# Attention and GRU kernel: the order of the first norm's powers and of two groups' block products

## What is computed

```python
block_repr = x.reshape(B, 8, 4, 256).sum(axis=2)          # 8 blocks of 4 tokens
keys = block_repr @ Wk.T;  keys = keys / rms(keys) * rms_weight
attn = softmax(keys @ q)                                   # over the 8 blocks
attended = sum(attn * block_repr)                          # one row per sequence
y = layernorm(x + attended @ Wo.T) * ln_gamma + ln_beta
```

## Time and profile before

| | |
|---|---|
| median of 3 executions | 449.07 us |
| lowest, highest | 448.49, 478.3 us |
| profiled execution | 448.79 us, its span 447.0 us |
| PE, DVE, ACT, POOL busy | 95%, 73%, 55%, 25% of the span |
| granted TensorE clock | 0.999 of full speed |

### The profile page before, as it was taken

The page is one execution under the profiler, slowest core; times in us unless marked ns, Lnnn a source line. Parts: engine busy times, 40 slices in busy tenths (PEclk is TensorE's granted clock), DMA queues, the critical chain, the costliest instruction groups (busy, mean ns, idle before and its releaser), DMA issues.

```text
span 447.0 us, 13398 instructions
## 1 busy us (share of the span) xinstructions
PE 422.7 (95%) x5424; PEld 347.7 (78%) x5424; DVE 325.2 (73%) x985; ACT 244.3 (55%) x558; POOL 109.9 (25%) x122
## 2 busy tenths in 40 slices
PE   8879899999999999999999899999999999999994
PEld 6436587787777777777777688899999999999984
DVE  3597688798788887878868945666677766777665
ACT  6255748568576586765876553444444444444341
POOL 7682434435134251342525300000000000000000
PEclk9999999999999999999999999999999999999999
DMA  8941513313133131331213100001010000000001
GB/s 287 408 165 44 151 36 89 88 51 90 63 91 88 57 96 54 93 88 49 84 31 92 28 1 1 1 2 47 1 47 14 36 24 26 23 25 25 24 25 70
DMA packets 34268, 30.36 MB, mean 68 GB/s; under 512 B 4128, under 2 KB 29344, under 8 KB 34208
## 3 DMA queue, kind: packets, MB, share of 16 engines
q1 hardware_dynamic: 34208, 29.51, 20.4%
HBM read 16.92 MB, written 8.39 MB: 57 GB/s over the span
## 4 chain that ended last, share of the span: by engine, by line
PE 70%; DVE 16%; ACT 7%; issue 4%; POOL 2%; DVEq 0%; POOLq 0%; ACTq 0%
PE ps_a L1252 10%; PE ps_s L1402 7%; PE ps_t L1402 6%; PE ps_o L1402 6%; PE ps_s L1458 5%; PE ps_t L1458 5%; PE ps_s L1301 4%; PE ps_m L1343 4%; PE ps_a L1458 4%; PE ps_m L1458 4%; DVE mx L943 3%; PE ps_o L1325 3%; PE ps_t L1314 3%; PE ps_m L1335 2%; DVE st L902 2%
## 5 line engine op out<-in xcount | busy, mean ns | idle before, releaser
L534 POOL TENSOR_TENSOR sc<-masked,mx 128x512 f32<-128x512 f32 x32 | 45.8, 1432 | 111.2 <-DVE mx L943 111.2
L1252 PE MATMUL ps_a<-yT_r,w_qkv_r 128*128 128x512 f32 x180 | 47.4, 405 | 2.1 <-POOL yT_r L491 1.2
L935 DVE COPY_PREDICATED masked<-kst,ps_s 128x512 f32<-128x512 int32 x64 | 44.0, 736 | 2.2 <-PE ps_s L1301 2.2
L742 ACT ACTIVATE zg<-ps_t,brz 128x128 f32<-128x128 f32 x64 | 20.0, 364 | 39.6 <-PE ps_t L1402 37.4
L1252 PEld LDWEIGHTS ps_a<-yT_r,w_qkv_r 128*128 128x128 f32 x180 | 32.2, 189 | 11.6 <-POOL yT_r L491 3.9
L943 DVE TENSOR_REDUCE mx<-masked 128x16 f32<-128x512 f32 x64 | 40.4, 672 | 0.0
L636 ACT ACTIVATE sc<-sc 128x512 f32<-128x512 f32 x64 | 37.1, 621 | 5.8 <-DVE sc L949 4.5
L1084 DVE SCALAR_TENSOR_TENSOR rg<-ps_o,vec,rg 128x128 f32<-128x128 f32 x64 | 19.4, 344 | 25.1 <-PE ps_o L1402 24.2
L565 ACT ACTIVATE pT<-ps_t 128x512 f32<-128x512 f32 x64 | 34.9, 601 | 4.1 <-PE ps_t L1314 3.2
L1402 PEld LDWEIGHTS ps_s<-hT,w_hh 128*128 128x128 f32 x256 | 33.0, 191 | 4.8 <-DVE hT L1102 2.8
L1343 PE MATMUL ps_m<-oT,w_p 128*128 128x128 f32 x256 | 34.9, 279 | 1.6 <-ACT oT L565 1.6
(11 more groups left out here) (157 smaller groups left out, 850.5 us busy)
## 6 DMA issues: line engine op xcount, KB each, us to landing
xf<-in_x_feat SPq DMA_DIRECT2D x8, 512.0 KB, 9.3
xg<-in_x_tok SPq DMA_DIRECT2D x8, 512.0 KB, 3.9
kbd<-kn SPq DMA_DIRECT2D x128, 32.0 KB, 1.8
v_dram<-vn SPq DMA_DIRECT2D x16, 256.0 KB, 3.5
vbd<-v_dram SPq DMA_DIRECT2D x64, 64.0 KB, 2.0
out_feat<-ost SPq DMA_DIRECT2D x16, 256.0 KB, 2.0
w_qkv<-in_wqkv SPq DMA_DIRECT2D x1, 768.0 KB, 9.3
w_ih<-in_wih SPq DMA_DIRECT2D x1, 768.0 KB, 12.9
```

The source lines that it names most:

```text
L534: nc.gpsimd.tensor_tensor(shifted, kept, m.unsqueeze(2).to_broadcast([P, NH // 2, S]), ALU.subtract).then_inc(sc_sub[1], 1)
L742: nc.scalar.activation(dst[:, c, :], gate_part(gate, c, t), ACT.Sigmoid, bias=brz[:, b0 + c:b0 + c + 1]).then_inc(done, 1)
L935: nc.vector.copy_predicated(kept, keep.unsqueeze(1).to_broadcast([P, NH // 2, S]), ps_s[:, h * 512:(h + 1) * 512].rearrange("p (h k) -> p ...
L1252: last = nc.tensor.matmul(bank, w_qkv_r[a][:, c, first_col + m * P:first_col + (m + 1) * P], yT_r[b][:, c, :], start=(a == b == c == 0), s ...
```

## The change

On **POOL** `block_sums(3)` moves behind the two powers of the first norm, `inverse_std_half(0)` and `(1)`. On **DVE** `token_stats_half` is split: the statistics proper keep the name, and the aggregation with the addition of epsilon is now `variance_half`. The second half's statistics move in front of `centre_half(0)`, the subtraction for the queries' weights (`rest_of_weights(2, Q_COLS)`) from in front of `whole_y` to behind `cond_shift(1)`. On **PE** `block_products(3)` moves from in front of the transposes to behind `first_keys`, with `keep_warm(2)` (two products whose result nobody reads) in its old place; `block_products(4)` moves from in front of `first_keys` to behind the queries; `spread_proj(1)` and the wait in front of it move before the second half of the queries. On **ACT** `cond_out(3)` and `cond_out(4)` follow their products: behind `k_chunk` and behind `q_chunk`. Nothing of the computation changes.

```diff
@@ -518,9 +518,9 @@
             inverse_rms(0)
             block_sums(1)
             block_sums(2)
-            block_sums(3)
             inverse_std_half(0)
             inverse_std_half(1)
+            block_sums(3)
             inverse_rms(1)
             block_sums(4)
             block_sums(5)
@@ -670,15 +670,15 @@
             cond_out(2)
             transpose_out(0, 0, yT_r[0], yt_hi)
             transpose_out(0, 1, yT_r[0], yt_hi)
-            cond_out(3)
             cond_exp(1)
             k_chunk(0, 0)
             k_chunk(0, 1)
-            cond_out(4)
+            cond_out(3)
             round_proj(1, proj_ps_1)
             act.wait_ge(w_ready, 1)
             q_chunk(0, 0)
             q_chunk(0, 1)
+            cond_out(4)
             v_half(0, 0)
             v_half(0, 1)
             normalise_tokens(1)
@@ -874,11 +874,14 @@
 
             def token_stats_half(h):
 
-                tiles = range(h * TH, (h + 1) * TH)
                 dve.wait_ge(z_done, h + 1)
-                for i in tiles:
+                for i in range(h * TH, (h + 1) * TH):
                     last = nc.vector.bn_stats(st[:, i, :], y[:, i, :])
                 last.then_inc(bn_done, 1)
+
+            def variance_half(h):
+
+                tiles = range(h * TH, (h + 1) * TH)
                 dve.wait_ge(bn_done, 2 * h + 1)
                 nc.vector.memset(carrier[:, 2:3], 0.0)
                 for i in tiles:
@@ -983,9 +986,11 @@
             rest_of_proj(0, proj_ps)
             add_proj_half(0, 0, ps_a)
             token_stats_half(0)
+            variance_half(0)
             add_proj_half(0, 1, ps_a)
+            token_stats_half(1)
             centre_half(0)
-            token_stats_half(1)
+            variance_half(1)
             cond_sums(1)
             centre_half(1)
             cond_mean(1)
@@ -994,7 +999,6 @@
                                     ALU.add).then_inc(b_out_done, 1)
             rest_of_weights(1, K_COLS)
             cond_scores(1)
-            rest_of_weights(2, Q_COLS)
             whole_y(1, 1)
             whole_y(0, 2)
             for c in range(C):
@@ -1003,6 +1007,7 @@
                 nc.vector.tensor_tensor(yT_r[1][:, c, :], yT[:, c, :], yT_r[0][:, c, :],
                                         ALU.subtract).then_inc(yt_lo, 1)
             cond_shift(1)
+            rest_of_weights(2, Q_COLS)
             cond_sums(2)
             cond_normalise(1)
             cond_sums(3)
@@ -1369,20 +1374,21 @@
             pe.wait_ge(l_wp, DMA)
             value_bias()
             block_products(2)
-            block_products(3)
+            keep_warm(2)
             transpose_first_y()
             cond_row(1)
-            block_products(4)
             pe.wait_ge(wqkv_lo, 1)
             first_keys()
+            block_products(3)
             cond_col(1)
             pe.wait_ge(wqkv_lo, 2)
             work_ahead(0, 1, 0)
             pe.wait_ge(b_out_done, 1)
             batch_proj(1, proj_ps_1)
-            work_ahead(0, 1, 1)
             pe.wait_ge(kw_out, 4)
             spread_proj(1, ps_t)
+            work_ahead(0, 1, 1)
+            block_products(4)
             pe.wait_ge(wqkv_lo, 3)
             work_ahead(0, 2, 0)
             work_ahead(0, 2, 1)
```

## The result

The changed kernel takes 457.18 us as median of 4 runs (455.95 to 457.65), the kernel before 450.97 (448.49 to 478.3). The ratio is 1.0137, 95% interval 1.0087 to 1.0186: slower by 1.4%. One execution of the kernel before, at 478.3 us, lies far outside all others; the median of 450.97 includes it. The profiled execution of the changed kernel took 457.65 us, with a span of 455.9 us and a granted clock of 0.983. Before, these were 448.79, 447.0 and 0.999. The forecast, 453.4 with 455.8 as upper end, had the direction and much too little of the size.

A forecast was written before the change was run, and what follows sets the result against it. PE was taken as the bound between first key and first score. DVE's late cond_sums(4) put group 1's yT_r +4.3 us, contention +0.3, so 448.8 + 4.6 = 453.4 us; range 450.6 to 455.8.

The forecast's parts named there:

- What bounds the kernel: Start-up: PE is the bound from first key to first score, busy 10.75 of 10.98 us; before the keys it waits.
- Part 1: First norm on POOL and DVE: second power 1.55 us earlier, keys start at about 28.1, 1.5 us earlier.
- Part 2: PE between keys and scores: two groups of products added there, first scores at 43.6 instead of 40.58, +3.0 us.
- Keys 3.4: PE's first item after the keys' start: the keys take 3.4 us, as before (3.36).
- second queries 1.5: PE behind spread_proj: the second half of the queries takes 1.5 us.
- group 4's products +1.85: PE behind the second queries: group 4's moved products add 1.85 us and end at 40.6.
- The contention term: POOL's block_sums(5) beside DVE's cond_sums(3) and select_blocks(1): slowed by 0 to 0.6 us, taken as 0.3.
- Part 3: DVE waits in cond_sums(4) until 41.3 with a queue behind it: group 1's yT_r +4.3 us, with contention +4.6.
- the slack of 0.4 us: ACT before group 1's yT_r, which could have come about 0.4 us earlier; taken off DVE's 4.7 us lateness.
- rival (a): DVE's lateness is hidden and only PE's +3.0 to 3.3 us counts, about 452 us; chance 0.17.
- Rival (c): TensorE's clock falls to 1.2 GHz after PE's pauses, keys take 5 to 6 us, 455.5 us; chance 0.05.
- Rival (b): Key transfers set the first score; the change is no slower and gains the keys' 1.5 us, 447.3 us; chance 0.08.

The follow-up runs named there:

- Experiment 4: Against the kernel before, only the moved products: PE and ACT as in the changed kernel, POOL and DVE as before; 457.45 us, ratio 1.0155.
- experiment 6: Changed kernel with 11 more warming products, and on DVE cond_sums(4) and cond_mean(2) moved behind mean_and_variance(1); 451.93 us, ratio 1.0008.
- experiment 1: Changed kernel with 11 more warming products, all where PE waits; 453.52 us, ratio 1.0064.
- experiment 10: Changed kernel with five warming products in front of the keys alone; 453.25 us, ratio 1.0035.
- experiment 11: Changed kernel with three warming products in front of group 1's transposes alone; 457.26 us, ratio 1.0113.

## Why the prediction was wrong

**What bounds the kernel: right.** PE's stretch between keys and scores has no room, and what is put there comes out at the end. Experiment 4 has the whole loss in the moved products.

**Part 1: the gain at the norm right, at the keys 0.7 us too good.** The second power came at 22.42 (22.1 forecast), block sums ended at 25.9 and not 25.2, because meeting DVE's subtraction they took 2.7 us instead of 2.2 (and that subtraction 1.17 us instead of 0.68), `whole_y` at 27.05 (26.4 to 26.8), the keys at 28.83 (28.1, upper end 28.9). Of these 0.7 us 0.3 lie ahead of the change: group 2's products began at 20.12 and not at 19.82.

**Part 2: the terms right, their clock wrong.** This is the step that failed. "Keys 3.4" measured 5.1 (28.83 to 33.92), "second queries 1.5" measured 2.5, "group 4's products +1.85" measured 2.34. That is 3.2 us in three terms up to the end of group 4's products, all from a granted clock of 0.52 and 0.65 of full in their stretches. Group 3's products (1.8), the first queries, the way of the projection (1.5) and the spreading stood as forecast. The contention term (0.3) measured 0.68, the wait for `ra`: above its upper bound. `cond_sums(3)` had to stand 3.99 us for group 3's products and their copy, and then its second part took 0.96 us instead of 0.41 beside POOL's block sums. First scores 48.16 against 43.6 forecast.

**Part 3: right.** From `cond_sums(4)` to group 1's normalisation it took 46.06 to 51.92 = 5.9 us, as before; the slack of 0.4 us was used up as said, and removing the dependence returned 1.6 us (experiment 6), against the 1.3 to 1.6 by which the forecast let this way exceed PE's own lateness (4.6 less 3.0 to 3.3). So rival (a) is out.

**Rival (c) was the case, at a chance of 0.05 and priced too low.** I let the keys alone fall, 455.5 us. The runs show two stretches on the path, 3.7 to 4.0 us together (experiments 1, 10 and 11). The step left out was to add up the pauses that the change would leave: ahead of the keys PE now stands for 3.75 us of 8.70 (20.10 to 28.80), where it stood for 2.82 of 9.80. The trace of before was read as evidence that pauses of 2.8 us in ten leave the clock at 1.00. It was one execution, and the median of three with its single profile didn't show that the kernel before stood at the edge: most of its executions take 1 to 4.6 us more at a lower clock. The earlier trace rows had a price of the right size, 634 against 379 ns, a factor of 1.7 as in the keys; but the profile's granted clock over those 7 us reads 1.00, so they don't show what I took them for. The rule of the Trainium skill, "TensorE: Matmul & The Clock Gate", What's actually happening, that the array falls to 1.2 GHz after idling, spoke for this rival. The trace after agrees with it: 0.52 in the keys, behind the three pauses. I had set both against one profile. Rival (b) is out for the changed kernel: SP's first issue is at 34.90, so by the forecast's own terms (8 x 0.64 and 1.8 us) the transfers are in at 41.8, and the first scores start at 48.16.

With the clock kept up the forecast of 453.4 us lies close to what was measured, 453.5 (experiment 1) and 453.3 (experiment 10). That it agrees to 0.1 us is luck: in the profiled execution of experiment 1, of 454.44 us, `cond_sums(4)` runs at 42.15 and not 41.3, and group 1's `y` at 48.01, the upper end of what was forecast. For the changed kernel itself it did not hold.

## What to carry to other kernels

Before moving matrix work out of a stretch in which TensorE waits, add up the pauses that it leaves, and price the next dense stretch at half clock; a profile at 1.00 is one draw, so look at the granted clock of every execution. Cheap products nobody reads, in the last pauses in front of a dense stretch, gave back 3.7 us of 457 here and made the kernel before 0.4% faster. And an engine's spare time is worth filling where it stands: work that hides in a wait costs its full length once it is moved to where there is none, and more, if another engine's queue reads its result first.

## What the hardware showed that was not expected

- The same pause near 1 us is followed by the low clock in one kernel and not in another. The wait of 1.01 us in front of `spread_proj(1)` is followed by a low stretch where the keys had run at the low level (profiles of experiments 4 and 11 and of the changed kernel) and by none where they had not (the profile of experiment 10). No run varied the pause alone, so what decides stays open.
- The low level shows in the matmuls of 512 columns as 5.26 against 3.03 us for twelve, a factor of 1.7; transposes and small matmuls suffer as well (eight transposes 1.56 against 1.09, scores 1.96 against 1.09, experiment 4 and the kernel before).
- DVE and POOL slow each other even in tiny instructions: adding epsilon to 128x2 took 0.75 us beside POOL's block sums and 0.17 without. A subtraction of 128x512 took 1.17 us beside them and 0.68 without, and POOL's two additions of 128x128 then took 1.32 us instead of 0.88. The Trainium skill, "GPSIMD Engine Reference", Key points, names instructions of VectorE with two SBUF inputs or in a two-port mode as those that contend. The subtraction has two such inputs, and the trace agrees; the addition of epsilon has one, and the trace doesn't show its mode.
